# Experts and state space in one block, with the rows of all elements kept on the chip

## The reference

```python
# experts: per token of all elements
logits  = x @ gate_w.T                      # 8 dynamic experts and a shared one
pick 4 of 8 (sparse mixer), top-p, at most CAP tokens an expert
y       = w_shared * shared(x) + sum_e w_e * expert_e(x)
x       = layernorm(x + y)
# state space: per element, 512 tokens in 4 chunks of 128
n       = rmsnorm(x)
z, xs, B, C, dt = split(n @ in_proj.T)
xs      = silu(causal_conv4(xs)); dt = softplus(dt + bias)
cs      = cumsum(dt * A)                    # decays inside a chunk and between chunks
y       = scan(dt * xs, B, C, exp(cs)) + D * xs
x       = layernorm(2 * x + (y * silu(z)) @ out_proj.T)
```

## Time and profile before

| | us |
|---|---|
| median of 3 runs | 3064.28 |
| lowest and highest run | 3058.69, 3073.77 |
| profiled execution, own time | 3060.05 |
| its span, first to last instruction | 3058.3 |
| experts' first PE instruction on rows | 1340.8 |
| last matmul of the experts ends | 1661.6 |
| first transpose of the state space | 1702.2 |
| last store of the state space issued | 2145.1 |

### The profile page before, as it was taken

One profiled execution on the slowest core, in us unless ns is written; L12 is line 12 of the kernel. 1 busy time (PEld: TensorE's weight loads), 2 busy tenths in 40 slices (PEclk: granted clock), 3 DMA queues, 4 the chain that ended last, 5 costly groups with the idle time before them and its releaser, 6 DMA issues. The chain is left out here.

```text
span 3058.3 us, 31620 instructions
## 1 busy us (share of the span) xinstructions
PE 2547.7 (83%) x11456; PEld 1497.1 (49%) x11456; DVE 1638.0 (54%) x3416; ACT 1386.3 (45%) x1989; POOL 319.9 (10%) x299
## 2 busy tenths in 40 slices
PE   5888888875888888879997688897588888887998
PEld 3555556552333333355454455565344445444555
DVE  4566555624666666716444587877555555541222
ACT  2333333311655555532222656553377777772221
POOL 0010001000000000000276000000211111000000
PEclk7899888967999998979898799998799999998999
DMA  2000000005333332240146221211300001001000
GB/s 72 7 14 14 14 14 14 7 7 153 57 65 63 63 64 55 46 150 0 35 72 104 94 70 42 84 42 42 101 7 28 28 28 35 14 14 62 14 21 21
DMA packets 113394, 140.81 MB, mean 46 GB/s; under 512 B 22004, under 2 KB 96004, under 8 KB 113240
## 3 DMA queue, kind: packets, MB, share of 16 engines
q1 hardware_dynamic: 98888, 123.97, 14.9%
q0 software_dynamic: 11904, 14.69, 3.0%
q10 hardware_dynamic: 2448, 0.14, 0.1%
HBM read 77.89 MB, written 35.39 MB: 37 GB/s over the span
## 5 line engine op out<-in xcount | busy, mean ns | idle before, releaser
L950 DVE TENSOR_REDUCE xattn_tops<-region 128x2 f32<-128x1024 f32 x256 | 306.3, 1220 | 126.0 <-PE region L734 125.9
L887 ACT ACTIVATE xattn_probs<-region 128x1024 f32<-128x1024 f32 x256 | 256.4, 1022 | 125.8 <-PE region L723 124.5
L2088 PE MATMUL region<-psi_fT 128*128 128x512 f32 x512 | 247.2, 622 | 24.7 <-DVE psi_low L2364 15.2
L122 PE MATMUL region<-gla_xT,weights_even 128*128 128x512 f32 (+1 forms) x416 | 206.4, 649 | 30.6 <-ACT gla_xT L214 30.6
L723 PE MATMUL region<-xattn_qs,xattn_ks 49*128 49x512 f32 x512 | 126.4, 495 | 61.8 <-DVE xattn_tops L950 31.4
L122 PE MATMUL region<-mamba_xT,weights_odd 128*128 128x512 f32 x320 | 157.6, 641 | 3.2 <-DVE mamba_xh L1927 3.2
L2088 PEld LDWEIGHTS region<-psi_fT 128*128 128x128 f32 x512 | 93.8, 196 | 135.2 <-issue 101.9
L122 PEld LDWEIGHTS region<-gla_xT,weights_even 128*128 128x128 f32 (+1 forms) x416 | 78.0, 196 | 144.5 <-issue 109.5
L131 PE MATMUL region<-weights_even,gla_work 128*128 128x256 f32 x512 | 123.4, 403 | 26.0 <-ACT gla_work L484 24.7
L752 PE MATMUL region<-xattn_probs,xattn_va 128*32 128x512 f32 x1024 | 141.8, 621 | 1.1 <-ACT xattn_o_T L914 1.1
L734 PE MATMUL region<-xattn_ks,xattn_qs 48*128 48x512 f32 x512 | 125.3, 488 | 13.9 <-DMA xattn_ks<-xattn_khi 9.5
(11 more groups left out here) (501 smaller groups left out, 5223.1 us busy)
## 6 DMA issues: line engine op xcount, KB each, us to landing
weights_even<-mamba_cs SPq DMA_DIRECT2D x32, 512.0 KB, 4.7
xattn_qs<-xattn_qhi SPq DMA_DIRECT2D x128, 64.0 KB, 2.3
xattn_ks<-xattn_khi SPq DMA_DIRECT2D x128, 64.0 KB, 2.3
moe_sums<-moe_picked SPq DMA_DIRECT2D x9, 512.0 KB, 8.6
gla_x<-in_x SPq DMA_DIRECT2D x8, 512.0 KB, 3.8
x_after_gla<-gla_res SPq DMA_DIRECT2D x8, 512.0 KB, 2.9
xattn_x<-x_after_gla SPq DMA_DIRECT2D x8, 512.0 KB, 4.1
xattn_ctxT<-in_ctxT SPq DMA_DIRECT2D x8, 512.0 KB, 4.4
```

The lines of the kernel that those rows point to most:

```text
L122: last = st.nc.tensor.matmul(o[0:m, i, :], w[:, c, col + i * P:col + i * P + m], rhs[:, c, :], start=c == 0, stop=c == kc - 1)
L887: A_(probs[:, p % 3, a, :, :], st.region(f"k{v}")[:], ACT.Exp).then_inc(st.emptying(f"k{v}"), 1)
L950: V.tensor_reduce(tops[:, n % 2, t, a::2], st.region(f"q{u}")[:], AX, ALU.max).then_inc(st.emptying(f"q{u}"), 1)
L2088: last = mm(o[:, a, :], fT[:, h, 0, t * P:t * P + P], fT[:, h, 1 + a, :], start=True, stop=True)
```

## The change

`moe_layer` now builds both layers in one block. The rows live in one buffer, `rows_kept`, for all 8 elements; the state space takes them from there and only its result is stored. What is gone: the experts' 8 stores of `x_after_moe`, the 8 loads of `mamba_x`, the barrier between the two blocks. The experts' other buffers are given up in the allocation (`ctx.close()`), so the state space's buffers lie at addresses that the experts used earlier. The state space is no longer a block but a `Program`: its list of events, and for each engine a function that executes one event. The list `beside` says how many of its events stand behind each `apply` of the experts; the rest follows behind the last.

```diff
+        xs, xT = both.enter_context(nc.sbuf_tensor("rows_kept", [P, B, NT, D], F32)), st.sb("xT", [B, DC, T])
...
+        ctx.close()
+        after = mamba_program(nc, both, A, K, psum, xs, x_out, next_weights, st)
...
+        beside = (1, 1, 1, 0, 1, 2, 2)
...
                 yield "apply", b - 1, 0
+                for k in range(sum(beside[:b - 1]), sum(beside[:b])):
+                    yield "next", k, 0
+            for k in range(sum(beside), len(after.work)):
+                yield "next", k, 0
...
             def _(sp):
...
-                for b in range(B):
-                    sp.wait_ge(st.sem("x_out"), b + 1)
-                    sp.dma_start(tokens(x_out, b), xs[:, b, :, :]).then_inc(st.sem("stored"), 16)
-                sp.wait_ge(st.sem("stored"), 16 * B)
+                next_weights.load(sp, A)
+                for what, b, i in work:
+                    if what == "next":
+                        after.sync(sp, *after.work[b])
+                sp.wait_ge(*after.stored)
...
-                for b in range(XS):
-                    load(b)
-                if K["next_weights"]:
-                    K["next_weights"].load(sp, A)
...
-                        sp.dma_start(tokens(x_out, b), xs[b % XS][:]).then_inc(st.sem("stored"), 16)
-                        if b + XS < B:
-                            sp.wait_ge(st.sem("stored"), 16 * (b + 1))
-                            load(b + XS)
-                sp.wait_ge(st.sem("stored"), 16 * B)
+            sp.dma_start(tokens(x_out, b), xs[:, b, :, :]).then_inc(st.sem("stored"), 16)
+        elif what == "xT" and b == 0 and K["next_weights"][1]:
+            sp.wait_ge(st.sem("normed"), 1)
+            K["next_weights"][1].load(sp, A)
...
-                        dve.wait_ge(st.sem(f"x_in{b % XS}"), 16 * (b // XS + 1))
-                        first.moments(dve, nth, x, rms=True)
+            dve.wait_ge(before.sem("x_out"), b + 1)
+            first.moments(dve, dve_nth, x, rms=True)
```

More of the change, by code:

```diff
@@ L74, in sem @@
         if name not in self.sems:
-            self.sems[name] = self.sems["keep"].enter_context(self.nc.semaphore(name))
+            self.sems[name] = self.pool.take(f"{self.label}_{name}", name.startswith(self.alone))
         return self.sems[name]
@@ L91, in filling @@
     def filling(self, name):
-        return self.sem("psum_full_{}{}".format(*self.place[name]))
+        return self.ring_sems.sem("psum_full_{}{}".format(*self.place[name]))
     def emptying(self, name):
-        return self.sem("psum_free_{}{}".format(*self.place[name]))
+        return self.ring_sems.sem("psum_free_{}{}".format(*self.place[name]))
     def full(self, name):
@@ L103, in zero_sems @@
     def zero_sems(self):
-        nums = sorted(s.num for n, s in self.sems.items() if n != "keep")
-        assert nums == list(range(nums[0], nums[-1] + 1)), nums
-        self.nc.multi_engine_barrier(list(self.nc.engines), sems_to_clear=range(nums[0], nums[-1] + 1))
+        self.nc.multi_engine_barrier(list(self.nc.engines), sems_to_clear=self.pool.given_back())
 def transposes(st, pe, name, src, ident):
@@ L219, in gla_layer @@
 def gla_layer(nc, A, K, psum, x_in, x_out, weights, SLOTS):
+    weights, = weights
     with ExitStack() as ctx:
@@ L1214, in _ @@
                         last.then_inc(st.filling(f"gue_end{b}"), 1)
+                    elif what == "next":
+                        after.tensor(pe, *after.work[b])
                     elif what == "down":
@@ L1258, in _ @@
                         A_(xT[:, b, :, :], st.region(f"down{b}")[:], ACT.Copy).then_inc(st.emptying(f"down{b}"), 1)
+                    elif what == "next":
+                        after.scalar(act, *after.work[b])
                     elif what == "exp":
@@ L1424, in _ @@
                         dve.wait_ge(*st.emptied("logits"))
+                    elif what == "next":
+                        after.vector(dve, *after.work[b])
                     elif what == "route":
@@ L1515, in _ @@
                 for what, b, i in work:
-                    if what == "gather":
+                    if what == "next":
+                        after.gpsimd(pool, *after.work[b])
+                    elif what == "gather":
                         gather(b)
@@ L2680, in build @@
         for i in range(run):
-            K["next_weights"] = weights[i + 1] if i + 1 < run else None
-            makers[LAYERS[i][0]](nc, A, K, psum, x, between[i], weights[i], SLOTS_OF[LAYERS[i][0]])
-            x = between[i]
+            if LAYERS[i][0] == "mamba":
+                continue
+            last = i + 1 if LAYERS[i][0] == "moe" else i
+            K["next_weights"] = [weights[k + 1] if k + 1 < run else None for k in range(i, last + 1)]
+            makers[LAYERS[i][0]](nc, A, K, psum, x, between[last], weights[i:last + 1], SLOTS_OF[LAYERS[i][0]])
+            x = between[last]
 SLOTS_OF = {"gla": 2, "xattn": 1, "moe": 2, "mamba": 1, "psi": 1, "ffn": 2}
```

823 lines of the change are left out of this document (415 added, 408 removed).

## The result

The changed kernel took 3032.68 us (median of 4 runs, 3025.01 to 3040.14), beside 3061.49 for the kernel before (4 runs, 3056.21 to 3073.77): ratio 0.9895, 95% interval 0.9859 to 0.9931, so 32 us faster with an interval of 21 to 43. (The ratio is not the quotient of the two medians, which lie 28.8 us apart.) Its profiled execution took 3040.14 us with a span of 3038.4; that of before took 3060.05 with 3058.3. The two executions with profiles thus lie 19.9 us apart, as forecast. The median, 3032.68, lies inside the stated range of 3030 to 3053; the ratio, set on the median of before, gives 3029.3, which lies under its lower edge.

The account below looks back on a forecast made before the run. No single bound overall; in the seam, a dependency chain with no engine busy. Lead 21.2 us less 1.2 for PE's clock gives gain 20: 3060.05 - 20 = 3040, stated as 3041, range 3030 to 3053.

Parts of the forecast that it names:

- The lead, steps 1 to 7: Seam, from apply 0 to ACT's copy of `bcT 0`: new order laid on old durations, copy starting 21.2 us earlier.
- DVE as cover and as bound: Seam: landings of accumulating DMAs covered by 5 us; DVE's lead at `cs 0` 23.5 us, so ACT is the late one.
- The term for PE's clock: Fill, PE idle some 3 us before `cb 0`: low clock makes `z 0` cost 0 to 2.55 us more, 1.2 taken.
- (b): State space's stride: a fixed partner or remaining barrier gives the lead back, end stays at 3060; chance 0.07.
- (d): State space's stride: PE's clock dips once more per element, 8 x 3.4 = 27 us lost, 3067; chance 0.05.
- (a): Seam: interleaved applies meeting late shifts or low clock eat 4 to 10 us, gain 10 to 16, about 3047; chance 0.16.
- (c): Seam and stride: DVE's 23.5 counts and freed DMA time advances fetches, gain 24 to 28, 3034; chance 0.12.
- The gain of 20 and the range: Whole kernel: the seam's lead kept to the end, gain 20 us, 3041 stated, range 3030 to 3053; chance 0.60.

Follow-up runs that it names:

- before_again: Unedited copy of the kernel before, built under its own name and timed against it: 3053.55 us beside 3059.59, ratio 0.9989.
- before_look2: Another unedited build of the kernel before, a further sample of its layers' lengths, timed against the kernel before: 3058.54 us, ratio 0.9985.

## Why the prediction was wrong, and where it was right

**The lead, steps 1 to 7: right.** Counted from apply 0, forecast and measured:

| | forecast | measured |
|---|---|---|
| apply 1 starts | 6.5 | 6.35 |
| `normed 0` starts | 10.1 | 9.85 |
| copy of xT starts | 13.9 | 13.60 |
| `dt 0` on PE starts | 15.2 | 14.92 |
| `dt 0` on DVE | 19.0 | 18.54 |
| apply 5 starts | 21.6 | 21.00 |
| `xs 0` on ACT starts | 25.5 | 25.00 |
| `bcT 0` starts | 34.8 | 33.86 |

The 1.0 us between 21.2 and 22.2 comes in two halves. Up to `xs 0` it is 0.5, spread over seven steps in which each semaphore was allowed 0.1. The other 0.4 is in the last step, where I added up durations: on ACT, when nothing is waited for, the next instruction starts before the one ahead has ended in the trace (the last apply starts at 1702.23 and takes 2.06, the copy of `bcT 0` starts at 1704.19). Each wait that I foresaw is in the rows, with its cause: the shift of apply 5 behind `dt 0` on DVE, `xs 0` nearly hidden (0.27), the table load on the path without any further pause behind it (1678.77, next instruction at 1680.07).

**DVE as cover and as bound: right.** DVE reaches `cs 0` 28.8 us after apply 0, a lead of 23.8 against 23.5 forecast; ACT is the late one. No landing is waited for. That the removed traffic is worth nothing by itself is shown, for this order of events, by the run with the traffic put back (33.9 against 33.9).

**The term for PE's clock: wrong.** I took 1.2 us of 0 to 2.55 off for `z 0`. It cost nothing: in all five profiles of the changed kernel `z 0` took 7.03, as in the earlier trace rows. The idle stretch ahead of `cb 0` was 2.21 to 2.23 us, not 3. The low level stayed where it was before the change, in `dt 0` and the first part of `xs 0` (9.75 to 10.06 in the five profiles, 9.26 to 10.01 in the four of before). In the seam the sum should have been 22.2 + 0, not 21.2 - 1.2.

**The rivals.** (b) is excluded by the stride, (d) too, with 348.8 us for seven elements against 348.2 and not 27 us more. (a) did not happen; its reason, ACT's chain of applies, is real all the same: another order takes 5.4 to 6.7 us out of the seam. (c), 24 to 28 us, fits the sum of the stages: from apply 0 to the first load of the next layer 482.6 us before (mean of four), 458.5 after (mean of five), 24.1 less. But its cause is not what (c) said: the seam has 22.2, the store of `csT 0` moved by the same 22.2 and not by more, and the last 2 us are the drain, whose length goes with the granted clock. The reason that I gave against (d), that the low clock follows an idle PE, does not hold in general: further down are windows at a low level with PE busy throughout.

**The gain of 20 and the range: here the prediction failed.** The mechanism held; the step that failed is the last one, from the chain to the time. The gain of 20 us was too small by its own terms: 21.2 for the seam measured 22.2, the 1.2 taken off for `z 0` measured 0, and behind the seam, where I added nothing, 1.9 came on top on the mean (24.1 in all). And the range gave the scatter of the comparison no term. Its lower edge, 3030, takes one execution less the 24 to 28 us of (c), and 2 us more; the untouched experts alone scatter from 326.7 to 339.6 us, and five comparisons of the same two kernels spread from 0.9895 to 0.9919. The first one fell at 3029.3.

The forecast was the profiled execution less 20 (3040, stated as 3041). The changed kernel's profiled execution is 19.9 less, and that is chance: from apply 0 to the next layer it took 25.7 us less, and untouched stages, 3.9 us longer ahead of the seam and 1.9 behind the state space, hid the rest. In the ratios the five comparisons give 0.9895, 0.9919, 0.9899, 0.9912 and 0.9901, on the mean 0.9905 or 29 us. The three copies of the kernel before, timed in the same way, gave 0.9989, 0.9987 and 0.9985 and not 1; set against their mean, 0.9987, the changed kernel is at 0.9918, which is 25 us and agrees with the 24.1 of the stages. I call this likely, not shown, since each of the three intervals holds 1. The medians say the same in their way: the five pairs lie 28.8, 21.6, 28.5, 22.2 and 22.8 us apart, 24.8 on the mean, and the three copies of before 6.0, 0.8 and 1.3. How much of the whole gain lies beyond the 22.2 of the seam stays open. The three runs before, which spread over 15 us, already showed that the range needed room for scatter.

## What to carry to other kernels

Lay the new order on old durations and count from an event that the change does not touch; here eight steps over 34 us came within 1 us. When a block's end goes, ask which in-order engine now carries the chain: here ACT, through the work that was meant as filler, and the places of the filler in its list were worth another 5 to 7 us of the seam, of which about 4 reached the next layer. Where untouched stages scatter by 10 us, judge a change of 20 us by the lengths of its own stages in several profiles, and give a range for the whole time that holds the scatter besides the mechanisms.

## What the runs showed of the hardware

**TensorE's clock in busy stretches.** The scatter of the untouched experts (326.7 to 339.6 us) goes with PE's granted clock. Here is the whole layer, load to apply 0, in two builds of the kernel before, before_again and before_look2, with the same 1092 rows on PE (columns as in the earlier trace rows):

```profile
1328.90:1655.55 326.65, 312.41 (x1092) 194.41 (x1092) 137.16 (x453) 71.78 (x127) 115.29 (x96) 0.91 0.34 72
1324.40:1663.90 339.50, 325.64 (x1092) 201.60 (x1092) 137.63 (x453) 71.85 (x128) 115.27 (x97) 0.87 0.32 69
```

At full speed that is 326.65 x 0.91 = 297 and 339.50 x 0.87 = 295 us, the same within the rounding. The profiles between them fit: 329.5 us at 0.90, 333.7 at 0.89, and 339.3 to 339.6 at 0.87 in both kernels. The largest part of the difference lies in one stretch of the layer, first in before_again, then in before_look2, whose layer began 4.5 us earlier:

```profile
1460.00:1480.00 20.00, 19.10 (x39) 7.06 (x38) 11.89 (x57) 3.97 (x12) 8.63 (x9) 0.83 0.16 46
1480.00:1500.00 20.00, 20.00 (x71) 11.69 (x70) 6.42 (x36) 5.35 (x12) 6.32 (x7) 1.00 0.18 52
```

```profile
1460.00:1480.00 20.00, 19.48 (x32) 6.99 (x31) 10.85 (x50) 3.42 (x10) 7.40 (x8) 0.67 0.14 40
1480.00:1500.00 20.00, 20.00 (x56) 12.23 (x55) 3.88 (x22) 3.07 (x8) 2.82 (x3) 0.66 0.09 26
```

PE is busy for 19 to 20 of each 20 us in both, and yet at 1.2 GHz for two thirds of these 40 us in the second. In work at full speed the difference is 20 x (0.83 - 0.67) + 20 x (1.00 - 0.66) = 10 us, of the 12.8 that the layer took longer. At the experts' start both kernels have PE busy without a gap at the low level; this is the changed one:

```profile
1350.00:1370.00 20.00, 20.00 (x97) 20.00 (x98) 0.00 (x0) 4.54 (x5) 0.00 (x0) 0.50 0.64 229
```

By the Trainium skill (TensorE: Matmul & The Clock Gate, Part 1: The HAM clock gate) the point at which the clock rises differs from run to run of one kernel; these windows, of two executions of the same code, agree, and show how much it can be worth: 13 us of 3060 in one layer.

**A short pause can cost the level, or not.** With 13 matmuls ahead, pauses of 1.19 and 2.02 us with 1.09 of work between them were followed by `dt 0` at 3.58, the low level. In the changed kernel a pause of 2.21 before `cb 0` was followed by `z 0` at 7.03, the high one. With 27 matmuls ahead that pause was 4.06, and `cb 0` took 2.07 instead of 1.16 and `z 0` 7.76.

**Landings of accumulating DMAs.** 512 KB landed every 2.64 to 2.71 us alone (one block, nothing interleaved), and 4.14 and 4.41 apart for the last ones of the kernel before, with stores beside them.

**A switch of ACT's table** cost 1.29 to 1.30 us from its start to the next start wherever in the seam nothing else was waited for.
